# Two more of a pair's sixteen heads moved through memory, their fours spent at the slot's end, the next states transposed later

## Time and profile before

| | |
|---|---|
| median of 3 runs (lowest to highest) | 2313.42 us (2313.23 to 2313.54) |
| the profiled execution's own time | 2312.53 us |
| its span | 2310.8 us |
| PE busy | 2213.7 us (96%) |
| DVE busy | 1809.3 us (78%) |
| ACT busy | 1684.7 us (73%) |
| POOL busy | 201.1 us (9%) |
| DMA, mean | 95 GB/s |

### The profile page before, as it was taken

One profiled execution on the slowest core, in us unless ns is written; L12 is line 12 of the kernel. 1 busy time (PEld: TensorE's weight loads), 2 busy tenths in 40 slices (PEclk: granted clock), 3 DMA queues, 4 the chain that ended last, 5 costly groups with the idle time before them and its releaser, 6 DMA issues.

```text
span 2310.8 us, 32320 instructions
## 1 busy us (share of the span) xinstructions
PE 2213.7 (96%) x10501; PEld 1560.7 (68%) x10501; DVE 1809.3 (78%) x5722; ACT 1684.7 (73%) x3243; POOL 201.1 (9%) x200
## 2 busy tenths in 40 slices
PE   5999999999999999999999999999999999999976
PEld 3766767767766777676676667766776776777643
DVE  5566687878788788887788797887878877766777
ACT  2444468777877768777787778787787877888786
POOL 0010110010100110001100101000100011001100
PEclk9999999999999999999999999999999999999978
DMA  6011025333172242432353430632415322200111
GB/s 221 10 37 55 10 96 158 106 115 124 28 219 87 74 142 78 155 124 65 109 154 97 137 119 29 203 107 73 135 53 184 110 64 93 69 19 19 37 42 37
DMA packets 115874, 219.30 MB, mean 95 GB/s; under 512 B 7768, under 2 KB 57212, under 8 KB 110332
## 3 DMA queue, kind: packets, MB, share of 16 engines
q1 hardware_dynamic: 115708, 217.24, 29.8%
HBM read 164.52 MB, written 52.69 MB: 94 GB/s over the span
## 4 chain that ended last, share of the span: by engine, by line
PE 79%; DVE 13%; ACT 4%; issue 2%; POOL 1%; DMA 0%; DVEq 0%; POOLq 0%; ACTq 0%
PE ffn L1246 22%; PE av L1163 14%; PE ffn L1235 12%; PE av L1235 12%; PE pT L1146 9%; PE av L1187 4%; PE av L1222 2%; DVE prob L778 2%; DVE prob L769 1%; ACT xs L553 1%; POOL rstd L470 1%; DVE lone L730 1%; PE trow L1125 1%; PE av L1273 1%; PE trow L1273 1%
## 5 line engine op out<-in xcount | busy, mean ns | idle before, releaser
L1246 PE MATMUL ffn<-w_sb,G 128*128 128x256 f32 x3072 | 740.5, 381 | 0.0
L1246 PEld LDWEIGHTS ffn<-w_sb,G 128*128 128x128 f32 x3072 | 560.8, 191 | 90.2 <-issue 24.3
L778 DVE CUSTOM_DVE_ANT_0 prob<-trow,mask 128x512 f32<-128x512 f32 x676 | 439.0, 685 | 34.3 <-PE trow L1125 19.5
L1146 PEld LDWEIGHTS pT<-ident,prob 128*128 128x128 f32 x2032 | 256.4, 144 | 147.6 <-issue 101.5
L1235 PE MATMUL ffn<-hT,w_sb 128*128 128x512 f32 x768 | 355.0, 595 | 0.9 <-issue 0.9
L1235 PE MATMUL av<-hT,w_sb 128*128 128x512 f32 x768 | 353.8, 593 | 0.0
L470 POOL TENSOR_TENSOR rstd<-veps,mhalf 128x4 f32<-128x4 f32 x127 | 167.2, 1317 | 2071.9 <-DVE veps L713 2071.9
L513 ACT ACTIVATE prob<-prob,s 128x512 f32<-128x512 f32 x484 | 331.5, 715 | 2.4 <-DVE nm L785 1.8
L1146 PE MATMUL pT<-ident,prob 128*128 128x128 f32 x2032 | 312.3, 278 | 19.8 <-DVE prob L841 7.5
L519 ACT ACTIVATE prob<-prob,nm 128x512 f32<-128x512 f32 x448 | 317.6, 712 | 0.0
L1163 PE MATMUL av<-xs,prob 128*128 128x257 f32 x1024 | 244.3, 380 | 3.9 <-ACT prob L524 3.9
(11 more groups left out here) (154 smaller groups left out, 2727.2 us busy)
## 6 DMA issues: line engine op xcount, KB each, us to landing
w_sb<-in_L_gnn_W SPq DMA_DIRECT2D x48, 1024.0 KB, 8.4
blocks_dram<-blocks SPq DMA_DIRECT2D x168, 256.0 KB, 4.2
prob<-blocks_dram SPq DMA_DIRECT2D x42, 1024.0 KB, 4.8
trow<-rows_dram SPq DMA_DIRECT2D x127, 256.0 KB, 3.2
adj_sb<-in_adj SPq DMA_DIRECT2D x16, 1024.0 KB, 7.0
xin<-in_x SPq DMA_DIRECT2D x16, 512.0 KB, 6.2
x0r<-in_x SPq DMA_DIRECT2D x16, 512.0 KB, 5.8
out<-o SPq DMA_DIRECT2D x15, 512.0 KB, 3.2
```

Of the source, the lines that this page charges most:

```text
L778: return v.tensor_tensor_reduce(out=out_[:, t, :], in0=targets, in1=mask[:, t, :], scale=1.0, scalar=LEAST, op0=ALU.add, op1=ALU.max, accu ...
L1146: last = te.transpose(pT[bank][:, j * P:(j + 1) * P], src[:, t, j * P:(j + 1) * P], ident[:])
L1246: last = te.matmul(ffn[part][:, at:at + D], G[:, f, t * P:(t + 1) * P], w2_sb[:, g // 2 % STAGES, f, :], start=f == 0, stop=f == FT - 1)
```

## The change

Heads 6 and 14 are added to those moved through memory, so 54 heads go that way instead of 42. Both, and heads 4 and 10 as before, have their DVE transpose ahead of the attention (s3, s0, s2, s4). In s3 and s0 the head that PE still turns (7, 15) is turned in the first product, where 6 and 14 stood; nothing is turned with pieces 6 to 9 there. In the slots with place 1 (s3 and s0, and s3 of the last pair) `attend_heads` moves from behind piece 10 to behind piece 13, `heads_back` from behind piece 12 to behind piece 14, and the next states are transposed behind piece 13 instead of 11; in the slots with place 2 (s4) they are transposed behind piece 12. ACT's `head_rows` and `transposed` move with them.

```diff
-BY_BLOCKS = (1, 2, 4, 5, 8, 10, 13)
-AHEAD = (2, 4)
+BY_BLOCKS = (1, 2, 4, 5, 6, 8, 10, 13, 14)
+AHEAD = (0, 2, 3, 4)
...
 def turned_ahead(g):
-    return [q for q in turned(g)[1:2] if moved(q) and g % SLOTS in AHEAD]
+    return [q for q in turned(g) if moved(q)][:1] if g % SLOTS in AHEAD else []

 def turned_behind(g):
-    return [q for q in turned(g)[1:] if moved(q) and q not in turned_ahead(g)]
+    return [q for q in turned(g) if moved(q)][len(turned_ahead(g)):]
+
+def turned_first(g):
+    return [q for q in turned(g)[:2] if not moved(q)][:1]
...
+def states_behind(place):
+    return {1: 3, 2: 2}.get(place, 1)
...
@@ scalar @@
-                        for q in heads[:1]:
+                        for q in turned_first(g):
                             turned_out(q, f - T)
...
-                        if not moved(q):
+                        if not moved(q) and q not in turned_first(g):
                             turned_out(q, t)
...
-                    if t == 0 and place == 1:
-                        head_rows(four)
-                    if t == 1:
+                    if t == states_behind(place):
                         for dt in range(DT):
                             transposed(dt, l2)
...
-                    if place == 2:
+                    if place in (1, 2):
                         head_rows(four)
@@ tensor @@
-                        for q in heads[:1]:
+                        for q in turned_first(g):
                             turn(q, f - T)
...
-                        if not moved(q):
+                        if not moved(q) and q not in turned_first(g):
                             turn(q, t)
...
                     piece(10 + t)
-                    if t == 0 and place == 1:
-                        attend_heads(four)
-                    if t == 1:
+                    if t == states_behind(place):
                         for dt in range(DT):
                             transpose_state(s2, dt)
-                    if t == 2 and place == 1:
-                        heads_back(four)
-                if place == 2:
+                if place in (1, 2):
                     attend_heads(four)
                 piece(14)
...
-                if place == 2:
+                if place in (1, 2):
                     heads_back(four)
                 piece(15)
```

## The result

| | before | after |
|---|---|---|
| median | 2313.23 us (5 runs) | 2323.73 us (5 runs) |
| ratio | | 1.0048, 95% interval 1.0033 to 1.0062 |
| profiled execution's span | 2310.8 us | 2322.6 us |
| PE busy | 2213.7 us | 2197.9 us |
| PE transposes of probabilities (L1146, L1154 after) | 2032 | 1840 |

The forecast was 2322.1 us. PE does less (192 transposes fewer) and the run is longer. In the chain that ended last PE's share falls from 79% to 69%, and DVE's and ACT's rise from 13% and 4% to 19% and 6%. Here are the page's chain and the two groups by shape that answer to the earlier trace rows.

What follows compares the result with a forecast made beforehand. PE held 79% of the chain of waits, but DVE set s4's attention and was late in s0. Terms 0.0 + 4.7 + 0.35 + 3.6 gave +8.7 us, forecast median 2322.1 us, range 2314 to 2329.

Steps and rivals of the forecast that it cites:

- PE's work removed: All pairs: two heads fewer turned by PE, 1.75 us each, 3.49 us a pair, 20.9 us of PE's stream.
- s3's gain is lost to the scores in s4: s3 into s4: PE ends s3 1.75 us earlier but waits for DVE-bound scores at first_target_row; gain 0.0.
- s4's third turn waits for turn 0's copy: s4: PE's turn 2 needs the bank freed by ACT's copy behind normalise; cost 0.79 us a pair, 4.7 over six.
- s0, head 14's transpose delays attend 2: s0: DVE is already late, attend 2 starts 1.94 us later; slot 0.6 longer, 3.6 over six.
- Transfers hidden: s0 and s3: moved heads' writes and reads land before the four needs them; head 14's cover 1.3 us, cost nothing.
- The clock: Rival: new PE waits lower the granted clock; in s0 about 2 us a pair, 12 in all, 2334 us; chance 7%.
- The sum: Whole run: 0.0 for s3, 4.7 and 0.35 for s4, 3.6 for s0, together +8.7 us.

Runs made afterwards that it cites:

- b_head6: Kernel before with head 6 alone moved through memory, ahead of s3's attention, and the new order in s3 alone; 2311.95 us, ratio to before 1.0000.
- d_masks: Changed kernel with the masks of the next pair's first graph made on DVE in s4 instead of s3; 2307.91 us, ratio to before 0.9981.
- a_states: Changed kernel with s4's next states transposed behind piece 11 again; 2319.48 us, ratio to before 1.0035.
- g_copy: Changed kernel with ACT's copy of the third head's turn 0 placed ahead of normalise in s4; 2316.17 us, ratio to before 1.0011.
- c_head14: Kernel before with head 14 alone moved through memory, ahead of s0's attention, and the new order in s0 alone; 2318.04 us, ratio to before 1.0021.
- f_ends: Changed kernel with the statistics ending the first network moved behind plus_bias in s0 on DVE; 2311.68 us, ratio to before 1.0002.
- o_order: Changed kernel with attend_heads behind piece 10, heads_back behind 12 and states behind 11 again in s3 and s0; 2332.84 us, ratio to before 1.0082.
- e_before_masks: Kernel before with the masks of the next pair's first graph made in s4 instead of s3; 2307.73 us, ratio to before 0.9981.
- k_before_two: Kernel before with masks made in s4 instead of s3 and the first network's statistics behind s0's attention; 2308.33 us, ratio to before 0.9978.
- h_all: Changed kernel with masks made in s4, first network's statistics behind s0's attention, and turn 0's copy ahead of normalise in s4; 2288.92 us, ratio to before 0.9898.
- m_stats: h_all with the first network's statistics ahead of plus_bias on DVE in s0; 2284.81 us, ratio to before 0.9874.

## Why the prediction was right, by its steps

*PE's work removed, 1.75 us a head.* Right: s3 is 1.76 us shorter.

*s3's gain is lost to the scores in s4.* Right, and shown twice: b_head6 (no gain) and d_masks (the gain appears when DVE's stretch is shortened). The wait at the scores was put at 1.6 to 1.7; it is 1.71 by distance.

*s4's third turn waits for turn 0's copy.* Right in mechanism (a_states, g_copy). The term was 0.79 a pair; it is 50.15 - 49.28 = 0.87, over the bound of +0.8. The wait at the third turn was 1.81 instead of 1.74 and that at the four 0.44 instead of 0.35.

*s0, head 14's transpose delays attend 2.* Right (c_head14, f_ends). The term was 0.6, which was also its upper bound; it is 0.8. I took the delay as 1.94; attend 2 starts 2.00 later, and the attends after a wait run slightly longer (attend 3's end 2.07 later). The wait at the states was put at 0.40; it was 0.41 by distance.

*Transfers hidden.* Right in the changed kernel. Head 14's read lands 38.4 to 40.0 us into the six s0 and the four starts at 41.23 or later, so the smallest cover is the 1.3 that was said; o_order shows what lay under it.

*The clock.* I gave 7% to its falling in s0. It did not happen as a rule but once: in one of six s0 of the profiled execution the wait at attend 2 was 2.24 us by distance instead of 2.0, the clock went to its lower level behind it and the slot took 48.99. In a_states and d_masks the same s0 has the same longer wait without the fall and takes 47.35 and 47.33, so the fall itself cost 1.6 to 1.7. PE's timeline there, and the granted clock (column after POOL) in that stretch:

```profile
1675.28 2.49 PE L1171 MATMUL av<-xin,prob 128*128 128x257 f32 x8 [2.08 <-DVE prob L856]
1677.56 1.91 PE L1254 MATMUL ffn<-w_sb,G 128*128 128x256 f32 x4
```

```profile
1677.00:1680.00 3.00, 3.00 (x8) 2.37 (x8) 1.60 (x5) 0.26 (x2) 0.00 (x0) 0.50 0.92 236
```

*The sum.* Forecast +8.7, measured +10.5 on the medians. Six pairs at 0.8 + 0.87 give 10.0, the last pair's s4 0.43 (forecast 0.35) and its s3 0.13 (0). Both sized terms came out too small, by 0.08 and 0.2 a pair, and that is the difference. The profiled executions differ by 11.8 as a whole and by 13.0 from the first slot to the start of the last: the 10.6, 1.9 more for the s0 above, 0.7 for one s4, 1.7 for the early fall shown below, and 2.0 less in the first pair.

## What to carry to other kernels

Before taking work off the engine that is busy 96% of the time, mark the places where it waits for another engine's chain, and look between which two of them the work lies: here the work between s3's and s4's attention was worth nothing until DVE's chain beside it was shorter, and then its whole price. Filling a wait with later work pays only if that work can itself run: look at what the moved instruction waits for in the other engines' written order. A step that is "hidden" on the helper engine is hidden by idle time at that very place: the same 2.31 us were free in s3 and cost 2.0 of PE's time in s0.

## What the runs showed of the hardware that was not expected

The same wait does not always give the same clock. In an early s0 PE waits 1.97 us for the states before and 1.98 after. The granted clock stayed at 1.00 in the one execution and fell in the other. The first row is before, the rest after:

```profile
323.93 1.09 PE L1222 MATMUL av<-ident,xs 128*128 128x128 f32 x8 [1.97 <-ACT xs L553]
```

```profile
321.16 1.68 PE L1230 MATMUL av<-ident,xs 128*128 128x128 f32 x8 [1.98 <-ACT xs L563]
322.63 3.67 PE L1254 MATMUL ffn<-w_sb,G 128*128 128x256 f32 x11
```

```profile
322.00:325.00 3.00, 3.00 (x10) 2.55 (x10) 0.43 (x4) 2.90 (x5) 0.00 (x0) 0.51 0.25 87
```

Between 300 and 2150 us the profiled executions had no stretch at the lower clock before and in d_masks, e_before_masks, k_before_two, h_all and m_stats, and one or two in all the others, ten in all. Each of the ten begins within 1.4 us of the end of a wait of 1.9 to 2.1 us of PE. But the early wait of 1.97 stands in all profiled executions but that of m_stats, and the clock fell there in five of twelve; behind the waits of 1.84 (in the row) at attend 2 it never fell. A fall in an s0 costs 1.6 to 1.7 us. What decides whether the clock falls stays open.

These falls are not the main source of the spread between runs. The time before the first slot and from the start of the last slot on, added up, ranges from 204.7 to 210.2 us over the thirteen profiled executions, although no edit is aimed at it. A difference of 2 us between two medians is therefore not read here without the slots.
